# Two-layer transformer block on one core: gated products ahead of the biased scores in even slots, both norms written by ScalarE, the first value product of a head group two slots later

## Time and profile before

| | |
|---|---|
| median of 3 executions | 2306.3 us (2303.06 to 2309.81) |
| the profiled execution | 2310.34 us |
| its span, first to last instruction | 2308.5 us |
| mean granted clock of TensorE | 0.971 |
| PE busy | 2078.7 us, 90% |
| PEld busy | 1355.0 us, 59% |
| DVE busy | 1635.0 us, 71% |
| ACT busy | 1400.3 us, 61% |
| POOL busy | 1147.4 us, 50% |

### The profile page before, as it was taken

The page is one execution under the profiler, slowest core; times in us unless marked ns, Lnnn a source line. Parts: engine busy times, 40 slices in busy tenths (PEclk is TensorE's granted clock), DMA queues, the critical chain, the costliest instruction groups (busy, mean ns, idle before and its releaser), DMA issues.

```text
span 2308.5 us, 52509 instructions
## 1 busy us (share of the span) xinstructions
PE 2078.7 (90%) x18761; PEld 1355.0 (59%) x18761; DVE 1635.0 (71%) x5384; ACT 1400.3 (61%) x3797; POOL 1147.4 (50%) x1800
## 2 busy tenths in 40 slices
PE   3888989989899998989989899998989999898988
PEld 1455655656566574655656566574655656566565
DVE  7557767677777767767677776767767677766756
ACT  1667566665756657566665756657566575756642
POOL 5675463745536454463645636454463745535220
PEclk7779999999999999999999999999999999999999
DMA  4000000000000000000000000000000000000000
GB/s 119 6 6 2 1 15 1 15 2 11 6 2 15 1 15 2 1 15 2 15 2 7 10 2 15 2 15 2 1 15 2 15 2 11 1 2 11 2 10 6
DMA packets 33542, 22.03 MB, mean 10 GB/s; under 512 B 2443, under 2 KB 32771, under 8 KB 33283
## 3 DMA queue, kind: packets, MB, share of 16 engines
q1 hardware_dynamic: 33283, 18.68, 2.8%
HBM read 14.48 MB, written 4.19 MB: 8 GB/s over the span
## 4 chain that ended last, share of the span: by engine, by line
PE 60%; DVE 16%; ACT 13%; issue 8%; POOL 4%; DVEq 0%; ACTq 0%; POOLq 0%
PE ps L1097 9%; PE ps L1168 9%; PE ps L1178 7%; PE ps L1237 7%; PE ps L1111 6%; ACT ring L921 4%; PE ps L1087 3%; PE ps L1066 3%; DVE ring L538 3%; ACT pb L930 3%; PE ps L1075 2%; PE ps L1222 2%; PE ps L1144 2%; PE ps L1195 2%; PE ps L1207 2%
## 5 line engine op out<-in xcount | busy, mean ns | idle before, releaser
L814 POOL TENSOR_SCALAR ring<-ring,row_rcp,tau_row 128x128 f32<-128x128 f32 (+3 forms) x1024 | 626.1, 618 | 824.4 <-DVE row_rcp L545 824.2
L921 ACT ACTIVATE ring<-ring,neg_max 128x128 f32<-128x128 f32 (+3 forms) x1024 | 572.2, 560 | 625.6 <-DVE neg_max L538 622.3
L1097 PE MATMUL ps<-identf,ring 128*128 128x128 f32 x2560 | 384.9, 288 | 17.9 <-ACT qkT L912 11.3
L930 ACT ACTIVATE pb<-ps 128x512 f32<-128x512 f32 x640 | 349.1, 585 | 23.9 <-PE ps L1097 16.8
L538 DVE CUSTOM_DVE_ANT_1 ring<-ps,bias_t 128x384 f32<-128x384 f32 (+1 forms) x496 | 287.2, 615 | 82.3 <-PE ps L1087 78.3
L1097 PEld LDWEIGHTS ps<-identf,ring 128*128 128x128 f32 x2560 | 280.1, 144 | 103.8 <-issue 62.6
L1168 PE MATMUL ps<-xn1T,eg_t 128*128 128x512 f32 (+1 forms) x480 | 265.1, 635 | 37.2 <-DVE h L592 36.9
L1237 PEld LDWEIGHTS ps<-ed_t,h 128*128 128x128 f32 (+1 forms) x1920 | 250.7, 191 | 74.7 <-issue 73.1
L1237 PE MATMUL ps<-ed_t,h 128*128 128x128 f32 (+1 forms) x1920 | 272.3, 278 | 0.0
L1178 PE MATMUL ps<-xn1T,eu_t 128*128 128x512 f32 (+1 forms) x480 | 259.3, 622 | 0.4 <-DVE h L599 0.4
L944 ACT ACTIVATE tanh_t<-ps 128x512 f32<-128x512 f32 (+2 forms) x304 | 171.9, 565 | 123.0 <-PE ps L1168 118.3
(11 more groups left out here) (161 smaller groups left out, 3208.2 us busy)
## 6 DMA issues: line engine op xcount, KB each, us to landing
x_t<-x SPq DMA_DIRECT2D x16, 256.0 KB, 2.8
x<-x SPq DMA_DIRECT2D x16, 256.0 KB, 2.8
out<-x SPq DMA_DIRECT2D x16, 256.0 KB, 2.3
bias_t<-bias SPq DMA_DIRECT2D x1, 1536.0 KB, 7.7
eg_t<-eg SPq DMA_DIRECT2D x1, 860.0 KB
eu_t<-eu SPq DMA_DIRECT2D x1, 860.0 KB
ed_t<-ed SPq DMA_DIRECT2D x2, 320.0 KB
ring<-inv_row SPq DMA_DIRECT2D x1, 256.0 KB, 2.7
```

The lines of the kernel that those rows point to most:

```text
L814: pool.tensor_scalar(e, e, row_rcp[:, m % 2, r:r + 1], tau_row[:, i, HG * g + r:HG * g + r + 1], ALU.mult, ALU.add).then_inc(p_ok.sem, 1)
L921: act.activation(e, e, ACT.Exp, bias=neg_max[:, n % 2, r:r + 1], scale=-1.0, accum_out=row_sum[:, n % 2, r:r + 1]).then_inc(exp_ok.sem, 1)
L930: act.activation(pb[:, c % NPB, :], bank(turn_bank(q)), ACT.Relu).then_inc(t_taken[q % 2].sem, 1)
L1097: last = pe.transpose(o[:, r * P:(r + 1) * P], ring_of(i, r)[:, k * P:(k + 1) * P], idf)
```

## The change

- DVE: in even slots `products` (silu and hidden) comes ahead of `biased`; in odd slots it stays where it was.
- Both norms: DVE now makes one small tile, shift = -mean * rstd for the four row tiles at once, and ACT writes the four tiles as Identity(rstd * x + shift) with scale and bias as operands, in the same slots as before (2, and 17 of layer 1), as the first of what lies beside. The wait for the turned fp4 tile of sequence b + 2 moves to ACT with it.
- The input's fp4 steps: each is one slot later (4, 5, 7, 8, 9, 10 in place of 3, 4, 6, 7, 8, 9), the turn at 11 stays.
- `HID_STEP`, the step sizes of the hidden values: slot 34 in place of 36.
- `blocks_before`: blocks of steps with i = 0 (the first step of a group) come four slots behind their transposes in place of two.

```diff
@@ -58,7 +58,7 @@
 TURN_X, FUTURE_X, QKV0, TURN_XQ = 5, 5, 7, 11
 GATE0 = (12, 14, 16, 18)
 STACK0 = (27, 45, 59, 69)
-HID_AMAX, HID_STEP, HID_SCALED = [p + 3 for p in GATE0], 36, (38, 39, 40, 41)
+HID_AMAX, HID_STEP, HID_SCALED = [p + 3 for p in GATE0], 34, (38, 39, 40, 41)
 HID_MAGIC, HID_ADD, HID_SUB, HID_MUL = (48, 50, 52, 54), (56, 58, 60, 62), (57, 59, 61, 63), (64, 66, 68, 70)
 TURN_H, FUTURE_V, FUTURE_Y = (ATT + 11, ATT + 13, ATT + 13, ATT + 15), ATT + 61, ATT + 63
 WO, WO_LAST, ADD_X1 = (L1 + 7, L1 + 8, L1 + 9, L1 + 11), L1 + 12, L1 + 14
@@ -152,7 +152,8 @@
 
     def blocks_before(self, f, s):
 
-        return self.blocks(*divmod(SLOTS * f + s - 2, SLOTS))
+        near, far = (self.blocks(*divmod(SLOTS * f + s - back, SLOTS)) for back in (2, 4))
+        return [blk for blk in far if STEPS[blk[1]][1] == 0] + [blk for blk in near if STEPS[blk[1]][1]]
 
 
 def build(nc, x, wq, wk, wv, wo, wo_pad, bias, tau, tau_col_in, wg, wu, wd, wqkv1, wout1, eg, eu, ed,
@@ -204,6 +205,7 @@
         stats = sb("stats", [P, 2, T, 6])
         moments = sb("moments", [P, 2, T, 2])
         rstd = sb("rstd", [P, 2, T])
+        shift = sb("shift", [P, 2, T])
         xn = sb("xn", [P, T, D])
         xq = sb("xq", [P, T * D])
         xn1 = xq[:, :].rearrange("p (t d) -> p t d", t=T)
@@ -287,6 +289,7 @@
         mom_ok = two("moments_ready", T)
         var_ok = two("variance_ready")
         rstd_ok = two("rstd_ready")
+        shift_ok = two("norm_shift_ready")
         xn_ok = two("xn_ready", T)
         x_step_ok = signal("x_fp4_step_ready", 3)
         x_scaled = signal("x_fp4_scaled")
@@ -491,11 +494,10 @@
                     dve.nop(nofuse=True)
                     dve.bn_aggr(moments[:, layer, t, :], stats[:, layer, t, :]).then_inc(mom_ok[layer].sem, 1)
 
-            def norm(b, layer, src, dst):
+            def norm_shift(b, layer):
                 dve.wait_ge(rstd_ok[layer].sem, rstd_ok[layer].at(b, 1))
-                for t in range(T):
-                    dve.tensor_scalar(dst[:, t, :], src[:, t, :], moments[:, layer, t, 0:1], rstd[:, layer, t:t + 1],
-                                      ALU.subtract, ALU.mult).then_inc(xn_ok[layer].sem, 1)
+                dve.scalar_tensor_tensor(out=shift[:, layer, :], in0=moments[:, layer, :, 0], scalar=-1.0, in1=rstd[:, layer, :],
+                                         op0=ALU.mult, op1=ALU.mult).then_inc(shift_ok[layer].sem, 1)
 
             def rope(b, layer, t):
 
@@ -699,7 +701,7 @@
             def urgent(b, p):
 
                 if p == 2:
-                    norm(b, 0, x_t, xn)
+                    norm_shift(b, 0)
                 if 0 <= p - QKV0 - 1 < T:
                     rope(b, 0, p - QKV0 - 1)
                 if p == ADD_X1:
@@ -711,9 +713,7 @@
                     dve.wait_ge(y_taken.sem, y_taken.at(b, 1))
                     norm_stats(b, 1, x1)
                 if p == ADD_X1 + 3:
-                    if has(b + 2):
-                        dve.wait_ge(t_ps.sem, plan.turn["xq", b + 2, 0] + 1)
-                    norm(b, 1, x1, xn1)
+                    norm_shift(b, 1)
                 if 0 <= p - QKV1 - 1 < T:
                     rope(b, 1, p - QKV1 - 1)
                 if 0 <= p - QKV1 - 4 < T:
@@ -726,10 +726,10 @@
                 if p == 0:
                     dve.wait_ge(x_in.sem, x_in.at(b, 16))
                     norm_stats(b, 0, x_t)
-                if p == 3:
+                if p == 4:
                     dve.wait_ge(xn_ok[0].sem, xn_ok[0].at(b, T))
                     fp4_steps(xn[:, :, :].rearrange("p t d -> p (t d)"), x_step, BX, x_step_ok, b)
-                if p == 6:
+                if p == 7:
                     dve.wait_ge(x_scaled.sem, x_scaled.at(b, 1))
                     fp4_magic(x_m[:, :], xq[:, :], x_magic, b)
                 if p in HID_AMAX:
@@ -753,14 +753,18 @@
                     dve.wait_ge(s_late.sem, N_LATE)
                 if f == 1 and s == 0:
                     dve.wait_ge(s_l1.sem, N_L1)
+                if s % 2 == 0:
+                    for b, p in plan.beside(f, s):
+                        products(b, p)
                 if has(f) and s % 2 == 0:
                     biased(f, s)
                     biased(f, s + 1)
                 for b, p in plan.beside(f, s):
                     for name, k in at(EXTRAS, p):
                         from_scores(b, name, k)
-                for b, p in plan.beside(f, s):
-                    products(b, p)
+                if s % 2:
+                    for b, p in plan.beside(f, s):
+                        products(b, p)
                 for b, p in plan.beside(f, s):
                     urgent(b, p)
                 for b, p in plan.beside(f, s):
@@ -820,18 +824,18 @@
             def beside(b, p):
                 if p == 1:
                     rstd_of(b, 0)
-                if p == 4:
+                if p == 5:
                     pool.wait_ge(x_step_ok.sem, x_step_ok.at(b, 3))
                     if has(b - 3):
                         pool.wait_ge(t_ps.sem, plan.turn["o1", b - 3, 0] + 1)
                     times_block(xq[:, :], xn[:, :, :].rearrange("p t d -> p (t d)"), x_step[:, 0, :], BX, x_scaled)
-                if p == 7:
+                if p == 8:
                     pool.wait_ge(x_magic.sem, x_magic.at(b, 2))
                     pool.tensor_tensor(xq[:, :], xq[:, :], x_m[:, :], ALU.add).then_inc(x_fp4.sem, 1)
-                if p == 8:
+                if p == 9:
                     pool.wait_ge(x_fp4.sem, x_fp4.at(b, 1))
                     pool.tensor_tensor(xq[:, :], xq[:, :], x_m[:, :], ALU.subtract).then_inc(x_fp4.sem, 1)
-                if p == 9:
+                if p == 10:
                     pool.wait_ge(x_fp4.sem, x_fp4.at(b, 2))
                     times_block(xq[:, :], xq[:, :], x_step[:, 1, :], BX, x_fp4)
                 if 0 <= p - QKV0 - 2 < T:
@@ -947,7 +951,19 @@
                 act.wait_ge(elum_ok.sem, elum_ok.at(b, t + 1))
                 act.activation(elu_m[:, t % 2, :], elu_m[:, t % 2, :], ACT.Exp).then_inc(elue_ok.sem, 1)
 
+            def norm(b, layer, src, dst):
+                act.wait_ge(shift_ok[layer].sem, shift_ok[layer].at(b, 1))
+                for t in range(T):
+                    act.activation(dst[:, t, :], src[:, t, :], ACT.Identity, bias=shift[:, layer, t:t + 1],
+                                   scale=rstd[:, layer, t:t + 1]).then_inc(xn_ok[layer].sem, 1)
+
             def beside(b, p):
+                if p == 2:
+                    norm(b, 0, x_t, xn)
+                if p == ADD_X1 + 3:
+                    if has(b + 2):
+                        act.wait_ge(t_ps.sem, plan.turn["xq", b + 2, 0] + 1)
+                    norm(b, 1, x1, xn1)
                 if p == TURN_X:
                     turned(("x", b, 0), xnT[:, :])
                 if p == TURN_XQ:
```

## The result

The changed kernel is slower: 2333.51 us (median of 4, 2332.83 to 2334.09) against 2304.99 us (median of 4, 2303.06 to 2309.81), a ratio of 1.012 with the interval [1.0103, 1.0138], or +28.5 us. The forecast was +13 us (2319), with its own range to 2332. So the direction is the one forecast and the size is half of what was measured: 2333.5 lies 1.5 us outside the forecast's own range, inside the whole range (to 2339), and nearer to rival D's 2341 than to 2319. The profiled execution took 2334.09 us around a span of 2332.3, 23.8 over the span of before; that the medians lie 28.5 apart and the spans 23.8 is because the profiled execution of before, 2310.34, was longer than each of its four timed ones.

The account below looks back on a forecast made before the run. TensorE (PE) sets the pace, busy 128.10 of 139.10 us a turn, with 11 us of stalls. Terms sum to +0.89 us a turn, x 15 = 13 us: 2319 us, forecast range 2308 to 2332, whole range 2272 to 2339.

Parts of the forecast that it names:

- rival D: Head of even slots: silu waits for tanh, 0.25 us more in six further slots, 1.5 a turn, 2341 us; chance 0.08.
- seven signs: Profile signs: 592/599 shorter, norm wait longer, qkT near 1.6, 1130 near 1.0, slot 5 waits gone, tile 0.27-0.40, DVE -57 us.
- rival A: Gates 27 and 47, slots 14 to 19: freed stalls stay freed, -2.05 us a turn, 2275 us; chance 0.18.
- Rival B: Slots 17 to 20: the norm off DVE frees PE's waits there, -0.71 us a turn, 2295 us; chance 0.14.
- C: Slots 17 to 20: it cancels, with half of Rival B's relief, +0.0, 2306 us; chance 0.22.
- Norm of layer 0: Slot 5: with this norm on ACT, PE's waits of 0.28 and 0.31 go, -0.59 us a turn.
- Slots 14 to 19: Three product stalls of PE go and return as a longer one ahead of the norm's turn, +0.25 us a turn.
- the ring: Slots 14 to 19: biased, exp, exp, tanh, silu, biased again sets the pace; two products in it add 1.04 us.
- Elsewhere: Slots 32 to 44 and 52 to 58: order costs nothing, covered by PE's work; +0.1 us a turn for slot 35.
- Slots 62 and 63: PE's 0.39 wait for the first biased score grows by 0.68, the copy returns about a third: +0.45 us a turn.
- Slots 26 to 29 and 46 to 48: Silu waits at gates 27 and 47 go but return behind scores and ACT's copies: +0.4 and +0.28 us a turn.
- The value product: Its wait for the attention copy stands ahead of gate(27), where PE only waits longer instead: 0 us a turn.

Follow-up runs that it names:

- e1: Only the new order of DVE's even slots (products ahead of the biased scores), on the kernel before: 2357.64 us, ratio 1.0223.
- e4: The whole change but with DVE's old order (products behind the biased scores), against the kernel before: 2285.27 us, ratio 0.9909.
- e2: Only both norms moved to ACT, with the input's fp4 steps one slot later, on the kernel before: 2284.83 us, ratio 0.9906.
- e7: e4 with only layer 1's silus at even slots ahead of the biased scores: 2283.83 us, ratio 0.9895 to the kernel before.
- e12: Only the norm of layer 0 on ACT, with the input's fp4 steps one slot later, on the kernel before: 2284.31 us, ratio 0.9913.
- e5: e4 with only layer 0's second products (slots 14, 16, 18, 20) ahead of the biased scores: 2298.62 us, ratio 0.9960 to the kernel before.
- e6: e4 with only layer 1's second (hidden) products ahead of the biased scores: 2309.48 us, ratio 1.0005 to the kernel before.
- e11: e4 with only the silus of slots 26 and 46 ahead of the biased scores: 2281.37 us, ratio 0.9903 to the kernel before.
- e3: Only the first value product of a group two slots later, on the kernel before: 2301.97 us, ratio 0.9991.

## Why the forecast was right, and where its size went wrong

**The mechanism held.** Five of its seven signs are in the trace: 592 and 599 under 30 us together (24.0), the wait for the norm longer with ACT as releaser (0.73 to 1.47), the wait of the stacked copy near 1.6 (as two waits, 0.99 + 0.68), slot 62's near 1.0 (1.03), and the 0.28 and 0.31 of slot 5 gone. The other two missed, both on the norm: a tile takes ACT 0.48, not 0.27 to 0.40, and DVE's busy time fell by 36.7, not 57. Stalls went and came back later and larger, and rival A (2275) is refuted by e1 and e4: the order never gained. Rival B (2295) wanted the norm to free 1.35 a turn in slots 17 to 20 and C (2306) half of that; e2 has 0.34 there. D (2341) comes nearest in time, but what it puts the loss down to costs 0.38 a turn (e7).

**Norm of layer 0, -0.59 a turn: too small, -1.05.** Both waits went, but a wait costs PE more than its bracket. First the row ahead of the two of the earlier trace rows in the kernel before, then slot 5 in e12:

```profile
986.44 0.83 PE L1237 MATMUL ps<-ed_t,h 128*128 128x128 f32 x6
```

```profile
836.91 0.83 PE L1252 MATMUL ps<-ed_t,h 128*128 128x128 f32 x6
...
837.58 0.73 PE L1136 MATMUL ps<-suffix_t,xn 128*128 128x3 f32 x6
...
838.17 0.38 PE L1090 MATMUL ps<-ident,qx 128*128 128x128 f16 x4
```

From the start of the suffix product to that of the next it is 0.59, where in the earlier trace rows it is 988.67 - 987.55 = 1.12: a difference of 0.53 for a bracket of 0.31. The busy time of the group, 0.73, contains 0.14 that the next group overlaps when it is ready; ahead of a wait nothing overlaps, and behind one the group itself is 0.07 longer (0.80 in the earlier trace rows). The wait ahead of it goes the same way: 837.58 - 836.91 = 0.67 against 987.55 - 986.44 = 1.11, a difference of 0.44 for a bracket of 0.28. That makes 0.97 out of brackets of 0.59; the turn is 1.05 shorter. The Trainium skill (TensorE: Matmul & The Clock Gate, section on single matmul latency) puts the drain of the array at about 175 ns for a bf16 matmul; by that the two waits would be worth 0.59 + 2 x 0.175 = 0.94 as an estimate, and the traces, with 0.97, agree.

**Slots 14 to 19, +0.25: the step that failed most, +0.92.** The order's part was right: two products in the ring, 1.04 forecast, 1.24 to 1.25 measured (after less e4, and e5). What failed is the relief by the norm: I had it give back 0.79, and it gave 0.31. ACT's tile took 0.48 and not 0.33, and DVE's small instruction 0.67 and not 0.17: the two together are 1.65 + 0.67 - 1.3 - 0.17 = 0.85 longer than I had them, more than the 0.48 that the relief fell short. So the lengths are enough to account for it, but that is worked out and not shown: no run had shorter ones with nothing else changed. For the tile an estimate by the Trainium skill (ScalarE: Activation LUTs, section on what ACT_TABLE_LOAD costs) was 0.48, and 1.64 for four; the traces agree with 481 ns and 1.64 to 1.65. I had taken the nearest rows instead, the plain copy and exp, which have no column operand and one.

**Elsewhere, +0.1: wrong.** The prediction says: "there I cost the order at nothing, the cover being PE's own work of a slot". The order costs 0.37 in slots 30 to 39 and 0.47 in slots 50 to 59. Of the first, 0.27 comes with the silus of layer 1 (e7) and 0.09 with its hidden products (e6); the second comes with the hidden products alone (e6 has 0.47, e7 0.00). These are places for which I had not gone through the timeline. The term for which I named no cover by a row was the one without cover.

**Slots 62 and 63, +0.45: +0.80.** The third that the copy was to give back did not come, and the wait's bracket grew by 0.64 for 0.80 of time.

**Slots 26 to 29 and 46 to 48, +0.4 and +0.28: too large, the order's part being +0.17 and +0.06.** By e7 and e11 these silus ahead of the scores cost about what they free. At slots 46 to 48 the waits grew only from 1.51 to 1.67: what PE no longer waits ahead of the gate, 1.11, it waits ahead of the two turns.

**The value product, 0: about -0.4 at full clock, and nothing in the time** (e3; slots 0 to 11 of e4 less e12 are -0.37). Slots 40 to 49 and 50 to 59, +0.14 and -0.36 in e4, are the same in e3.

**What the sum left out: the clock.** The terms add to +0.89 a turn against +1.15 measured, 13 and 17 us; that these are so near each other is luck, since misses of -0.84 to +0.67 in the single stretches mostly cancel. The remaining 11 of the 28.5 are the 0.43 a turn at half clock (6 us), 0.4 at the two ends of the span, and the 4.7 by which the medians lie further apart than the spans, the profiled execution of before having had the low clock told above. The trace of before has such stretches, and the prediction took the clock as full.

## What to carry to other kernels

An instruction moved ahead in an in-order queue delays everything behind it by its full length, unless the engine would have waited there. So ask at each place what its cover is, by a row, and treat a place without one as a loss. Here the 19 products moved are 12.3 us long a turn (4 x 0.52 + 15 x 0.68), 3.1 of it was not covered, and for 42 us of PE's stalls that went (66.2 in e4, 24.0 after) the kernel paid 48 us. A wait of TensorE that goes wholly is worth more than its idle time, 0.16 and 0.22 us more at the two of slot 5; these two, with brackets of 0.59 us a turn, brought the gain, and the far larger stalls at the gates only changed their place. And where a bundle is tried, its parts are worth timing alone: here one part alone gives all of the time that the others reach together, and another hides it.

## What the hardware showed that I had not expected

**The clock falls behind the same few stalls, but not in every turn.** Slots 19 and 20 of the kernel after, the same work in two turns (columns as in the earlier trace rows):

```profile
1027.60:1031.00 3.40, 3.40 (x20) 1.83 (x19) 2.13 (x8) 2.02 (x8) 1.32 (x3) 0.50 0.00 0
1169.00:1172.40 3.40, 3.40 (x28) 2.13 (x25) 2.13 (x9) 2.02 (x7) 1.31 (x3) 1.00 0.00 0
```

In the first, right behind the 1.47 us wait for the norm, the granted clock is 0.50, the 1.2 GHz level, and PE starts 20 matmuls where it starts 28 in the other at 2.4 GHz. A turn with such a stretch is about 1.4 us longer (138.76 against 137.41 and 139.92 against 138.57 above). In the kernel before most begin near slot 28 or 42, in the kernel after near slot 18 to 20 or 50. Where one meets the gate of slot 27 in the kernel before, two matmuls take 2.08 us that take 1.12 in the earlier trace rows, behind the same wait:

```profile
894.76 2.08 PE L1168 MATMUL ps<-xn1T,eg_t 128*128 128x512 f32 x2 [1.32 <-DVE h L592]
```

Which turns have one, the runs do not explain: e12 kept all of those silu waits and had 3 stretches in turns 1 to 14, where the kernel before had 12. The Trainium skill (TensorE: Matmul & The Clock Gate, section on a second HAM failure mode) tells of a kernel whose short idle times between groups of matmuls make the clock swing between its two levels; these traces agree as far as the swings go, 12 of them in these turns before and 16 after.

**The same small instruction of DVE takes 0.16 us at slot 2 and 0.67 at slot 17** (rows above). The view of its line in the kernel after, with the least, the median and the greatest duration in ns:

```profile
L499 DVE SCALAR_TENSOR_TENSOR shift<-moments,rstd x32: 161/165/742, 7.9 to 2255.3; 128x4 f32<-128x4 f32 x32
```

The traces show what goes with it. In all 15 long instances (671 ns or more) an instruction of POOL had begun 62 to 108 ns before, and DVE's ended 5 to 17 ns behind the end of POOL's: the last of the three in the row at 1023.01 runs from 1024.51 to 1025.28, and the shift ends at 1025.29. In the 17 short ones (165 ns at most) POOL was idle, twice, or had begun only 35 to 37 ns before (the row at 991.81). No run moved POOL's instruction, so that it is the cause is not shown.
